# Dense layer with 4-bit weights: two of eight groups kept as whole numbers, scaled behind the product

## The reference

```
x = x + attention(layernorm(x), ctx) @ Wo          # 32 heads of 128, rope, mask, softmax
x = x + layernorm(x) @ W + bias                    # the dense layer
W[k, n] = scales[g, n] * (nibble(qweight)[k, n] - nibble(qzeros)[g, n]),   g = k // 128
```

## Time and profile before

| | |
|---|---|
| time, median of 3 runs | 2245.61 us (2245.2 to 2246.51) |
| profiled execution, its own time | 2246.42 us |
| its span | 2244.6 us |
| TensorE busy | 2219.1 us, 99% |
| VectorE busy | 1373.5 us, 61% |
| ScalarE busy | 1052.8 us, 47% |
| GpSimd busy | 1392.6 us, 62% |

### The profile page before, as it was taken

How to read it: one execution, slowest core, us unless ns; L and a number is a source line. 1 busy time by engine, 2 the same in 40 slices (tenths; PEclk the granted TensorE clock), 3 DMA queues, 4 the chain that set the end, 5 groups by cost and what they waited for, 6 DMA issues and landing times.

```text
span 2244.6 us, 33169 instructions
## 1 busy us (share of the span) xinstructions
PE 2219.1 (99%) x10562; PEld 1862.3 (83%) x10562; DVE 1373.5 (61%) x2536; ACT 1052.8 (47%) x2296; POOL 1392.6 (62%) x980
## 2 busy tenths in 40 slices
PE   8999999999999999999999999899999999999999
PEld 6888888888888888788888888778888888888887
DVE  4782575777777778877777777523675445453532
ACT  3232123767666767766666666622333333331100
POOL 1320453788888889888888888765663354454210
PEclk9999999999999999999999999999999999999999
DMA  6766675687888889887888888687654564451111
GB/s 248 269 230 217 237 269 200 204 255 242 242 260 237 245 251 271 252 262 237 242 249 248 241 250 243 205 320 259 199 187 151 162 197 151 158 193 69 47 47 47
DMA packets 299899, 476.71 MB, mean 212 GB/s; under 512 B 23568, under 2 KB 195888, under 8 KB 299824
## 3 DMA queue, kind: packets, MB, share of 16 engines
q1 hardware_dynamic: 285744, 440.12, 62.5%
q10 hardware_dynamic: 13312, 33.56, 3.8%
q0 software_dynamic: 768, 2.10, 0.3%
HBM read 303.70 MB, written 171.98 MB: 212 GB/s over the span
## 4 chain that ended last, share of the span: by engine, by line
PE 91%; DVE 3%; POOL 3%; DMA 1%; issue 1%; ACT 1%; SPq 0%; DVEq 0%; ACTq 0%; POOLq 0%
PE ps L241 22%; PE ps L242 22%; PE ps L243 22%; PE ps L814 9%; PE ps L815 8%; PE ps L816 8%; PE ps L838 1%; POOL rope_tmp L1561 1%; DMA left_scratch<-s_buf 0%; POOL s_buf L1561 0%; DVE rope_tmp L1170 0%; DVE rope_tmp L1171 0%; DVE rope_tmp L1169 0%; POOL wraw L1646 0%; ACT wq_t L882 0%
## 5 line engine op out<-in xcount | busy, mean ns | idle before, releaser
L241 PE MATMUL ps<-act_t,wq_t 128*128 128x512 f32 x1280 | 500.3, 391 | 1.3 <-DVE act_t L1232 0.6
L242 PE MATMUL ps<-act_t,wq_t 128*128 128x512 f32 x1280 | 499.6, 390 | 0.0
L243 PE MATMUL ps<-act_t,wq_t 128*128 128x512 f32 x1280 | 498.0, 389 | 0.0
L1634 POOL TENSOR_TENSOR b_parts<-wraw,b_parts 128x512 fp32r<-128x512 f32 x112 | 199.2, 1779 | 262.6 <-ACT b_parts L1032 262.6
L814 PE MATMUL ps<-b_parts,a_parts 128*128 128x512 f32 x896 | 349.1, 390 | 1.7 <-POOL b_parts L1634 1.4
L815 PE MATMUL ps<-b_parts,a_parts 128*128 128x512 f32 x896 | 348.6, 389 | 0.0
L816 PE MATMUL ps<-b_parts,a_parts 128*128 128x512 f32 x896 | 348.6, 389 | 0.0
L1339 DVE TENSOR_TENSOR a_parts<-xring,a_parts 128x1024 fp32r<-128x1024 f32 x112 | 147.7, 1318 | 303.7 <-ACT a_parts L1027 303.7
L1616 POOL TENSOR_TENSOR q_t<-pt_raw,q_t 128x1024 fp32r<-128x1024 f32 x124 | 302.5, 2440 | 46.3 <-ACT q_t L1010 43.5
L1561 POOL TENSOR_TENSOR rope_tmp<-rope_tmp 128x512 f32<-128x512 f32 x144 | 193.4, 1343 | 182.9 <-DVE rope_tmp L1171 182.8
L1027 ACT ACTIVATE a_parts<-xring 128x1024 fp32r<-128x1024 f32 x112 | 118.7, 1060 | 389.6 <-PE ps L816 385.5
(11 more groups left out here) (132 smaller groups left out, 4367.8 us busy)
## 6 DMA issues: line engine op xcount, KB each, us to landing
sq_scratch<-scores SPq DMA_DIRECT2D x124, 512.0 KB, 3.0
pt_raw<-sq_scratch SPq DMA_DIRECT2D x496, 128.0 KB, 4.0
xring<-left_scratch SPq DMA_DIRECT2D x112, 512.0 KB, 3.7
left_scratch<-s_buf SPq DMA_DIRECT2D x64, 640.0 KB, 5.2
wraw<-in_L_xattn_Wq SPq DMA_DIRECT2D x64, 512.0 KB, 4.6
wraw<-in_L_xattn_Wo SPq DMA_DIRECT2D x64, 512.0 KB, 4.5
v_scratch<-kv_t ACTq DMA_DIRECT2D x32, 512.0 KB, 3.3
k_scratch<-kv_t ACTq DMA_DIRECT2D x32, 512.0 KB, 4.8
```

Source lines behind the costliest of these rows:

```text
L241: eng.matmul(dst, lh, rh, start=(k == first), stop=False)
L242: eng.matmul(dst, lh, rl, start=False, stop=False)
L243: mm = eng.matmul(dst, ll, rh, start=False, stop=(k == last))
L1634: pool.tensor_tensor(b_parts[:, s % 2, 1, :], wraw[s % 2][:, 0:NW], b_parts[:, s % 2, 0, :].bitcast(F32), ALU.subtract).then_inc(right_lo, 1)
```

## The change

The order of the weight rows becomes the natural one: group g is the weight rows 128 g to 128 g + 127, with one row of zeros and one of scales. SyncE loads for each group 16 rows of packed words, each to eight partitions, and its zeros and scales, to all partitions. Partition p needs the nibble p % 8: VectorE shifts by a column of shifts (`shift_col`, a new input) and masks in a second instruction, and it unpacks the zeros for each group anew.

Groups 0 and 1 (`WHOLE`) are not multiplied by their scales. Their weights are whole numbers from -15 to 15, which the high part holds exactly, so they have no low part and take two products instead of three. Each gets its own bank per half (banks 6 and 7). VectorE multiplies this bank by the scales into one of four `partial` buffers, and GpSimd adds that to the row, behind the bias; VectorE adds the bank of the other six groups (`SPLIT`) last. The normalized row is read without a stride.

```
-        DENSE_AT = (25, 28, 34, 37, 40, 43, 54, 57)
+        WHOLE = (0, 1)
+        SPLIT = tuple(g for g in range(KT) if g not in WHOLE)
+        DENSE_AT = (24, 28, 34, 38, 42, 54, 58, 70)
 @block.sync
+            def load_group(g):
+                if g == 0:
+                    sp.dma_start(shift_col[:, :], shifts).then_inc(shifts_in, 16)
+                else:
+                    sp.wait_ge(wf_full, g)
+                rows16 = P // KT
+                sp.dma_start(packed, qweight[g * rows16:(g + 1) * rows16, :].rearrange("r (a n) -> r a n", a=1)
+                             .broadcast_to([rows16, NIB, E])).then_inc(dense_in, 16)
+                sp.dma_start(zero_words[:, :], qzeros[g:g + 1, :].rearrange("g (a w) -> g a w", a=1)
+                             .broadcast_to([1, P, E // NIB])).then_inc(dense_in, 16)
+                if g not in WHOLE:
+                    sp.dma_start(scale_rows, scales[g:g + 1, :]...).then_inc(dense_in, 16)
+            def load_scales():      # behind the last step's loads
+                sp.wait_ge(m_added, 8 * sum(spared(m)[0] for m in range(7)))
+                for j, g in enumerate(WHOLE):
+                    sp.dma_start(whole_scales[:, j, :], scales[g:g + 1, :]...).then_inc(scales_in, 16)
...
                 if s == 20:
-                    sp.dma_start(packed, qweight).then_inc(dense_in, 16)
-                if s == 21: ...scale_rows...
-                if s == 22: ...zero_words...
+                    load_group(0)
+                if s - 3 in DENSE_AT[:-1]:
+                    load_group(DENSE_AT.index(s - 3) + 1)
 @block.tensor, dense(r)
                 for n in range(2):
+                    for j, g in enumerate(WHOLE):
+                        q = 4 * r + 2 * n + j
+                        if q < 2:
+                            pe.wait_ge(m_out, 48 + 6 + j + 1)
+                        else:
+                            pe.wait_ge(x_scaled, q - 1)
+                        dst, cols = ps[:, 6 + j, :], slice(n * NW, (n + 1) * NW)
+                        pe.matmul(dst, x2t[r % 2][:, 0, g, :], w_parts[:, g, 0, cols], start=True, stop=False)
+                        pe.matmul(dst, x2t[r % 2][:, 1, g, :], w_parts[:, g, 0, cols], start=False, stop=True).then_inc(x_done, 1)
...
-                             range(KT), 0, KT - 1).then_inc(ffn_done, 1)
+                             SPLIT, SPLIT[0], SPLIT[-1]).then_inc(ffn_done, 1)
 @block.scalar
-                if s - 1 in DENSE_AT:
+                if s - 1 in DENSE_AT and DENSE_AT.index(s - 1) in SPLIT:
                     dense_hi(DENSE_AT.index(s - 1))
 @block.vector, dense_full(g)
+                dve.wait_ge(dense_in, 48 * (g + 1) - 16 * sum(i <= g for i in WHOLE))
+                for i in range(NIB):
+                    dve.tensor_scalar(zeros_f...[:, :, i], zero_words[:, :], BITS * i, 2 ** BITS - 1, ...).then_inc(z_step, 1)
...
-                dve.tensor_scalar(w_full.bitcast(I32), packed, BITS * i, 2 ** BITS - 1, ALU.logical_shift_right,
-                                  ALU.bitwise_and).then_inc(dq_step, 1)
+                dve.tensor_tensor(w_full.bitcast(I32), packed, shift_col[:, :].broadcast_to([P, E]),
+                                  ALU.logical_shift_right).then_inc(dq_step, 1)
+                dve.tensor_scalar(w_full.bitcast(I32), w_full.bitcast(I32), 2 ** BITS - 1, None,
                                   ALU.bitwise_and).then_inc(dq_step, 1)
+                if g in WHOLE:
+                    dve.tensor_tensor(w_parts[:, g, 0, :], w_full.bitcast(I32), zeros_f, ALU.subtract).then_inc(wf_full, 1)
+                else: ...subtract zeros, multiply by scale_rows, as before...
+            def scale_part(q):
+                dve.wait_ge(x_done, q + 1)
+                if q >= 4:
+                    dve.wait_ge(x_added, q - 3)
+                n, j = q // 2 % 2, q % 2
+                dve.tensor_tensor(partial[q % 4], ps[:, 6 + j, :], whole_scales[:, j, n * NW:(n + 1) * NW],
+                                  ALU.mult).then_inc(x_scaled, 1)
             def y_normalize(r):
-                dve.tensor_scalar(xn[r % 4].rearrange("p (j r) -> p j r", j=NIB),
-                                  rows[:, r, :].rearrange("p (r j) -> p j r", j=NIB),
+                dve.tensor_scalar(xn[r % 4], rows[:, r, :],
...                                (in the loop over r, for n in range(2):)
+                    for j in range(2):
+                        scale_part(4 * r + 2 * n + j)
                     dve.wait_ge(ffn_done, 2 * r + n + 1)
-                    if n == 0:
-                        dve.wait_ge(biased, r + 1)
+                    dve.wait_ge(x_added, 4 * r + 2 * n + 2)
 @block.gpsimd
+            def add_part(q):
+                r, n = q // 4, q // 2 % 2
+                dst = rows[:, r, n * NW:(n + 1) * NW]
+                pool.wait_ge(x_scaled, q + 1)
+                pool.wait_ge(biased, r + 1)
+                if q % 2 == 1:
+                    pool.wait_ge(x_added, q)
+                pool.tensor_tensor(dst, dst, partial[q % 4], ALU.add).then_inc(x_added, 1)
+            add_bias(0)
             for r in range(16):
+                for q in range(4 * r, 4 * r + 2):
+                    add_part(q)
+                if r + 1 < 16:
+                    add_bias(r + 1)
+                for q in range(4 * r + 2, 4 * r + 4):
+                    add_part(q)
```

More of the change, by code:

```diff
@@ L66, in rope_table, with build @@
     return np.concatenate([cos, cos, sin, -sin], axis=1)
-def build(nc, x, ctx_t, x_tiles, x_pieces, pos, mask, wq, wk, wv, wo, qweight, qzeros, scales, bias, table, ident, out):
+def build(nc, x, ctx_t, x_tiles, x_pieces, pos, mask, wq, wk, wv, wo, qweight, qzeros, scales, bias, table, ident, shifts,
+          out):
     x_rows = x.rearrange("b s e -> (b s) e").rearrange("(r p) e -> r p e", p=P)
@@ L179, in build @@
         packed, scale_rows = dense[:, 0, :].bitcast(I32), dense[:, 1, :]
+        whole_scales = spare[:, 4:8, :].rearrange("p (g a) n -> p g (a n)", g=2)
+        partial = [spare[:, i, :] for i in range(4)]
         zeros_f, w_full = dense[:, 2, :].bitcast(I32), dense[:, 3, :]
@@ L572, in _ @@
             attention(15, 1, last=True)
+            def load_group(g):
[9 more added lines that the diff above has]
+                if g not in WHOLE:
+                    sp.dma_start(scale_rows, scales[g:g + 1, :].rearrange("g (a n) -> g a n", a=1)
+                                 .broadcast_to([1, P, E])).then_inc(dense_in, 16)
+            def load_scales():
+                sp.wait_ge(m_added, 8 * sum(spared(m)[0] for m in range(7)))
+                for j, g in enumerate(WHOLE):
+                    sp.dma_start(whole_scales[:, j, :], scales[g:g + 1, :].rearrange("g (a n) -> g a n", a=1)
+                                 .broadcast_to([1, P, E])).then_inc(scales_in, 16)
             for s in range(4, STEPS):
@@ L1092, in _, with dense_hi @@
             attention(15, last=True)
-            def dense_hi(i):
-                if i == 0:
+            def dense_hi(g):
+                if g == SPLIT[0]:
                     for s in range(2):
@@ L1476, in dense_lo, with dense_full @@
-            def dense_lo(i):
-                dve.wait_ge(wf_hi, i + 1)
-                dve.tensor_tensor(w_parts[:, i, 1, :], w_full, w_parts[:, i, 0, :].bitcast(F32),
-                                  ALU.subtract).then_inc(wf_lo, 1)
+            def dense_full(g):
+                before = sum(i < g for i in SPLIT)
+                dve.wait_ge(dense_in, 48 * (g + 1) - 16 * sum(i <= g for i in WHOLE))
+                for i in range(NIB):
+                    dve.tensor_scalar(zeros_f.rearrange("p (w i) -> p w i", i=NIB)[:, :, i], zero_words[:, :],
+                                      BITS * i, 2 ** BITS - 1, ALU.logical_shift_right,
+                                      ALU.bitwise_and).then_inc(z_step, 1)
+                if before > 0:
+                    dve.wait_ge(wf_lo, before)
+                if g == 0:
+                    dve.wait_ge(shifts_in, 16)
+                dve.tensor_tensor(w_full.bitcast(I32), packed, shift_col[:, :].broadcast_to([P, E]),
+                                  ALU.logical_shift_right).then_inc(dq_step, 1)
+                dve.wait_ge(dq_step, 3 * g - sum(i < g for i in WHOLE) + 1)
+                dve.tensor_scalar(w_full.bitcast(I32), w_full.bitcast(I32), 2 ** BITS - 1, None,
+                                  ALU.bitwise_and).then_inc(dq_step, 1)
+                dve.wait_ge(dq_step, 3 * g - sum(i < g for i in WHOLE) + 2)
+                dve.wait_ge(z_step, NIB * (g + 1))
+                if g in WHOLE:
+                    if g == WHOLE[0]:
+                        for i in range(2):
+                            dve.wait_ge(o_stored[i], 32 * 32)
+                        dve.wait_ge(sums_stored, 64 * 16)
+                    dve.tensor_tensor(w_parts[:, g, 0, :], w_full.bitcast(I32), zeros_f, ALU.subtract).then_inc(wf_full, 1)
+                else:
```

(23 more changed lines are left out.)

26 lines of the change are left out of this document (9 added, 17 removed).

## The result

The changed kernel takes 2268.1 us (median of 4) against 2246.1 us; the ratio is 1.0094, 95% interval 1.0082 to 1.0106. Forecast were 2257 us, range 2244 to 2268, slower. The sign was right and so was the place of the forecast losses; the size, 11.6 us, was about half of the 22.1 that came. The time lies at the very end of the range (the median 0.1 us past it, the ratio just inside), and outside the forecast's own range of 2250 to 2264.

The account below looks back on a forecast made before the run. TensorE, without slack in the step stage and dense layer, was taken as the bound: 2246.42 - 5.1 (dense layer: 14.5 saved, 9.4 waited) + 16.7 (dequantization) = 2258.0, or 2257.2 us as median; range 2244 to 2268.

Parts of the forecast that it names:

- The bursts: Step stage: VectorE's eight dequantizations, lengthened by waits for GpSimd, make TensorE wait for the left remainder, 16.7 us together.
- M4 and M3: Blocks of the step stage with right sums, steps 34, 38, 42, 70: TensorE waits 2.65 us each, 10.6 together.
- the whole groups: Dequantizations at steps 24 and 28, without multiplication: TensorE waits 1.45 us each, 2.9 together.
- M5: Block of the step stage without right sums, steps 54 and 58: TensorE waits 1.6 us each, 3.2 together.
- Rival three: Dequantization: the zero instructions don't wait for GpSimd, so bursts cost only 6.8 us; 2247 us in all, chance 0.12.
- rival one: Dequantization: waits between VectorE and GpSimd vanish, bursts are hidden, only the dense layer changes; 2240.5 us, chance 0.10.
- The early dense rows: Dense rows 1 to 4: TensorE waits for VectorE's scaling, 1.8, 3.4, 2.2 and 2.0 us, 9.4 together.
- The loop of the dense stage: Each dense row: VectorE to GpSimd and back takes 10.8 us, just fitting the row's 10.86; no loss.
- Loads: SyncE's loads per group: late right halves bounded at 0 to 8 us in all, taken as 0.

Follow-up runs that it names:

- e1: Changed kernel with all eight groups split, so no whole groups and no scaled parts in the dense stage: 2269.5 us, ratio 1.0101.
- e2: Changed kernel with each group's dequantization laid over three steps, groups farther apart, same instructions and loads: 2245.9 us, ratio 0.9997.
- e5: Changed kernel with the same eight dequantization bursts, four of them moved to blocks without right sums: 2257.3 us, ratio 1.0047.
- e9: Changed kernel with only the dense stage's row statistics and inverse deviation moved behind the scaling of a half row: 2255.7 us, ratio 1.0048.
- e6: Changed kernel with GpSimd adding the next row's bias after the four parts of a row, not between them: 2261.0 us, ratio 1.0069.
- e7: Changed kernel with dequantization over three steps and reordered dense stage, plus 14 idle-purpose bn_stats in each of six steps: 2237.8 us, ratio 0.9964.
- e8: Changed kernel with dequantization over three steps and reordered dense stage, plus 17 idle-purpose bn_stats in each of six steps: 2253.0 us, ratio 1.0030.

## Why the prediction was right, and where it was short

*The bursts (16.7 us forecast; 13.1 + 0.16 for each of the eight = 14.4 measured, and 1.0 at two late right halves).* The 0.16 is there because a row counts a wait from the end of the last matmul, 0.39 us after its start, while the next one would have started after 0.227. Right in mechanism and order; e1, e2 and e5 show it from three sides. M4 and M3 came at 2.3 to 2.8 against 2.65, the whole groups at 1.2 and 1.6 against 1.45. Too high only for M5: 0.2 instead of 1.6 each. There the reading of the earlier trace rows failed. I took the merged row to show that only the first zero instruction waits for GpSimd. In short windows the traces tell better; the first two zero instructions in the kernel before, then in the changed one at step 34 and at step 54 in M5:

```profile
1568.99 2.63 DVE L1507 TENSOR_SCALAR dense<-zero_words 128x128 int32<-128x128 int32 x2
1629.30 2.64 DVE L1508 TENSOR_SCALAR dense<-zero_words 128x128 int32<-128x128 int32 x2
1750.50 1.53 DVE L1508 TENSOR_SCALAR dense<-zero_words 128x128 int32<-128x128 int32 x2
```

In M4 the second one waits too, for L1707, and it did in the kernel before, for L1646: the forecast could have known. In M5, where GpSimd has no such instruction, it doesn't, and all is 1.1 us earlier; the subtraction (1754.67) is then ahead of GpSimd's L1695 (1755.36), not behind it. So these strided instructions wait for GpSimd as contiguous ones do, each of them. The disagreement with the Trainium skill that the prediction saw (page "SBUF — State Buffer", section "Who interferes with whom") was none: the Trainium skill's page "VectorE: DVE Perf Modes", section "Mode 2×_2P", asks for operands in SBUF and an even (or equal) outermost dimension in that mode, not for unit stride. The trace agrees as far as it goes: both instructions wait. Rival three, which rested on it, is thereby out, and so is rival one: the waits are there, 1.1 us each.

*The early dense rows (9.4 forecast; 8.5 and 0.16 for each of four, 9.1, measured).* Right as a place and a mechanism; e9 removes most of it. That the sum fits to 0.3 us is partly luck: rows 1 to 4 were forecast at 1.8, 3.4, 2.2 and 2.0 and waited 1.4, 3.4, 0.8 and 2.8, so row 3 was too high and row 4 too low. (For row 1 the prediction's own times, 7.2 to 7.5 against 5.86, give 1.3 to 1.6, not 1.8.)

*The loop of the dense stage (a turn of 10.8 us forecast, 11.2 measured; nothing forecast in all, 1.3 us measured).* Named, and mis-sized. One turn, VectorE and then GpSimd (VectorE's rows for the second half are left out):

```profile
2145.15 0.69 DVE L1604 TENSOR_TENSOR rows<-ps,rows 128x512 f32<-128x512 f32 x1 [3.17 <-POOL rows L1760]
2145.76 1.28 DVE L1586 TENSOR_TENSOR a_parts<-ps,a_parts 128x512 fp32r<-128x512 f32 x2
2146.96 0.80 DVE L1552 TENSOR_SCALAR dense<-rows,mean_var,inv_std 128x1024 f32<-128x1024 f32 x1
2147.68 1.28 DVE L1546 TENSOR_TENSOR spare<-ps,spare 128x512 f32<-128x512 f32 x2
2156.35 0.69 DVE L1604 TENSOR_TENSOR rows<-ps,rows 128x512 f32<-128x512 f32 x1 [3.16 <-POOL rows L1760]
```

```profile
2148.44 1.30 POOL L1760 TENSOR_TENSOR rows<-rows,spare 128x512 f32<-128x512 f32 x1 [3.39 <-DVE spare L1546]
2149.91 1.29 POOL L1760 TENSOR_TENSOR rows<-rows,spare 128x512 f32<-128x512 f32 x1 [0.17 <-POOL rows L1760]
2151.15 2.40 POOL L1750 TENSOR_TENSOR rows<-rows,bias_rows 128x1024 f32<-128x1024 f32 x1
2153.51 1.29 POOL L1760 TENSOR_TENSOR rows<-rows,spare 128x512 f32<-128x512 f32 x1
2154.97 1.28 POOL L1760 TENSOR_TENSOR rows<-rows,spare 128x512 f32<-128x512 f32 x1 [0.17 <-POOL rows L1760]
```

From 2145.15 to 2148.44 VectorE needs 3.29 (3.1 in the sum), from there to 2156.35 GpSimd 7.91 (7.4 and 0.3 of signals). Missing were the second part's wait for the first (`x_added`, 0.2 us, twice a row) and 0.07 of the normalization (it takes 0.80 us, not 0.65 to 0.75). TensorE feels the longer turn late: it starts each of the rows 6 to 9 still 10.9 us after the one before and only the four behind them 11.2 after, which is 1.3 us. The sum had only 0.1 us of room in a row of 10.86; a term so close to deciding should have been put down as a range. e6 removes it by taking the bias out of the loop.

*The lower clock (nothing forecast, 8.5 measured).* This is the term that the sum lacks, and the largest miss. "TensorE has no slack" was priced as the wait and nothing more. With it the account all but closes: steps 15.4 + 5.1 = 20.5 of 20.8 measured between the first zero instruction and the first transposition; dense - 14.5 + 9.1 + 3.4 + 1.3 = - 0.7 of + 0.1, so 0.8 stay open; 1.9 from the attention, which nothing in the change explains. e7 and e8 show that waits alone bring the lower clock about: four of e8's five waits of 2.75 us did, none of e7's shorter ones.

*Loads:* hardly anything, as forecast; two waits of 0.4 us and 0.3 us at late right halves. GpSimd's own waits for them rose from 8.7 us (1500 to 2051) to 31.6 (1500 to 2074), nearly all of it hidden. In e1, e5 and e6, whose loads are the same up to there, one such wait of TensorE at 1596 to 1598 us was 0.6, 0.8 and 2.0 us.

## What to carry to other kernels

Where the bounding engine has no slack, the unit to plan with is one step: a burst on a side engine must end within the step, counting each wait for the shared port, and cutting it into three pieces was worth 22 us here at no cost that shows. Work added to a row needs to be traced as a loop through all engines that hand it on, not as a sum per engine; what isn't needed in the loop (here the bias and the statistics) belongs behind it. And a wait of TensorE of 2 us or more may cost 1.7 us beyond itself.

## What the runs showed of the hardware that was not expected

- In the steps and the dense stage of all twelve traces, TensorE waited 18 times for 2.6 to 3.4 us, and at 17 of these a stretch at 1.2 GHz began in the last microsecond of the wait or up to 1.6 us behind it; so it did at 6 of 16 waits of 2.3 us, at 2 of 3 of 1.9 to 2.0, and at none of 40 from 0.7 to 1.8. A stretch cost 1.7 us (one in e2 was twice as long). The last three waits of the attention, 36 in all, were of 1.3 to 2.6 us, and only 7 had one, none of the three longest among them. Why 2.29 us had it at step 70 and not at step 34 is open.
- A strided one-input VectorE instruction of 128x128 waited 1.1 us for a GpSimd instruction, and the next one for the next (2.63 us for two in the kernel before, 2.64 in the changed one; 1.53 where GpSimd had only one).
- The contiguous normalization of 128x1024 takes 0.80 us, with a stride of eight it took 1.26.
